# Folding keys into the query weights of four latent attentions, moving the mask test to other engines, and running batch 0's last attention inside the last decoder layer

## What is computed

```python
# L0 and L3 (softmax over the 512 tokens, not over the 77 keys)
q = x @ Wq + bq;  k = ctx @ Wk + bk;  v = ctx @ Wv + bv
w = softmax(q @ k.T / sqrt(128), axis=tokens)
x = layernorm(w @ v + x) * gamma + beta
# L1 (ordinary cross attention, one head)
x = x + softmax((x@Wq+bq) @ (ctx@Wk+bk).T / sqrt(128)) @ (ctx@Wv+bv) @ Wo + bo
# L2: six layers, 16 heads of 64
t = mha(ln(t), ln(t), self weights, mask 512 x 512) + t
t = mha(ctx, ln(t), cross weights, mask 77) + t
t = t + relu(ln(t) @ w1 + b1) @ w2 + b2
```

## Time and profile before

| | us |
|---|---|
| median of 3 runs | 1139.71 (1138.81 to 1141.12) |
| the profiled execution, whole | 1137.97 |
| its span, first to last instruction | 1136.1 |
| PE busy / ACT / DVE / POOL | 1043.2 / 773.5 / 751.3 / 385.2 |
| prologue, to the first decoder norm | 0 to 74.57 |
| one steady layer (out job at 224.81, next at 395.89) | 171.08 |
| last residual sum to the end | 1112.17 to 1136.1 |

### The profile page before, as it was taken

How to read it: one execution, slowest core, us unless ns; L and a number is a source line. 1 busy time by engine, 2 the same in 40 slices (tenths; PEclk the granted TensorE clock), 3 DMA queues, 4 the chain that set the end, 5 groups by cost and what they waited for, 6 DMA issues and landing times.

```text
span 1136.1 us, 21080 instructions
## 1 busy us (share of the span) xinstructions
PE 1043.2 (92%) x5374; PEld 659.5 (58%) x5374; DVE 751.3 (66%) x4546; ACT 773.5 (68%) x3453; POOL 385.2 (34%) x398
## 2 busy tenths in 40 slices
PE   5469999999999999999999999999999999999874
PEld 3346655656655656655656655666655666655532
DVE  2736578856678855678765678765678765678634
ACT  2128689856689856689856589856589856589821
POOL 2003344322344322354322354322354323354310
PEclk9659999999999999999999999999999999999987
DMA  8320110000410000310000410000410000000000
GB/s 240 50 70 1 51 33 1 1 1 11 115 33 2 1 1 2 121 35 1 2 1 1 121 37 2 1 1 2 121 36 1 2 1 1 20 1 1 1 0 19
DMA packets 37263, 32.45 MB, mean 29 GB/s; under 512 B 10768, under 2 KB 32528, under 8 KB 35984
## 3 DMA queue, kind: packets, MB, share of 16 engines
q1 hardware_dynamic: 37136, 31.03, 9.8%
HBM read 30.49 MB, written 0.52 MB: 27 GB/s over the span
## 4 chain that ended last, share of the span: by engine, by line
PE 83%; DVE 10%; issue 3%; ACT 2%; DVEq 1%; DMA 0%; SPq 0%
PE sum L856 23%; PE S L826 21%; PE T L836 11%; PE W L740 4%; PE W L682 4%; PE W L746 4%; PE W L669 2%; PE W L720 2%; PE W L699 2%; DVE Pb L1192 2%; PE W L735 2%; DVE XN L1045 1%; PE W L651 1%; PE W L660 1%; DVE stats L1034 1%
## 5 line engine op out<-in xcount | busy, mean ns | idle before, releaser
L986 ACT ACTIVATE Pb<-Pb,mn 128x128 f32<-128x128 f32 (+1 forms) x1536 | 560.9, 371 | 65.0 <-DVE mn L1192 65.0
L547 POOL TENSOR_TENSOR Pb<-Pb,rsum 128x512 f32<-128x512 f32 (+2 forms) x336 | 325.1, 969 | 600.6 <-DVE rsum L1200 600.1
L986 ACT ACTIVATION_READ_ACCUMULATOR Pb<-Pb,mn 128x1 f32 x1536 | 294.8, 192 | 0.0
L836 PEld LDWEIGHTS T<-ident,Pb 128*128 128x128 f32 (+2 forms) x1296 | 163.7, 147 | 153.9 <-issue 114.8
L1192 DVE CUSTOM_DVE_ANT_0 Pb<-S,late_bias 128x128 f32<-128x128 f32 x768 | 175.5, 285 | 110.5 <-PE S L826 109.8
L826 PE MATMUL S<-GV,XT 128*128 128x512 f32 x384 | 197.2, 600 | 1.4 <-DVE mn L1192 0.8
L836 PE MATMUL T<-ident,Pb 128*128 128x128 f32 (+2 forms) x1296 | 197.4, 273 | 0.0
L856 PE MATMUL sum<-PT,GV 128*128 128x512 f32 x384 | 192.4, 593 | 0.0
L1209 DVE COPY PT<-T 128x512 f32<-128x512 f32 (+1 forms) x240 | 157.3, 656 | 43.6 <-PE T L836 42.1
L1192 DVE CUSTOM_DVE_ANT_0 Pb<-S,cross_bias 128x77 f32<-128x77 f32 x768 | 132.4, 233 | 42.8 <-PE S L826 38.8
L856 PE MATMUL sum<-PT,Vc 128*128 128x512 f32 (+2 forms) x264 | 134.5, 599 | 0.0
(11 more groups left out here) (136 smaller groups left out, 1071.8 us busy)
## 6 DMA issues: line engine op xcount, KB each, us to landing
sakv<-in_L_xattn_sa_kv SPq DMA_DIRECT2D x6, 1024.0 KB, 5.3
caow<-in_L_xattn_ca_ow SPq DMA_DIRECT2D x132, 32.0 KB, 2.3
saq<-in_L_xattn_sa_q SPq DMA_DIRECT2D x6, 512.0 KB, 6.1
caq<-in_L_xattn_ca_q SPq DMA_DIRECT2D x6, 512.0 KB, 8.1
cakv<-in_L_xattn_ca_kv SPq DMA_DIRECT2D x6, 512.0 KB, 9.4
saow<-in_L_xattn_sa_ow SPq DMA_DIRECT2D x6, 512.0 KB, 4.2
w<-in_L_xattn_ff_w SPq DMA_DIRECT2D x12, 256.0 KB, 3.1
GV<-in_mask_BxSxS_ik SPq DMA_DIRECT2D x1, 2048.0 KB, 10.1
```

The costliest lines, as they stand in the source:

```text
L547: nc.gpsimd.tensor_tensor(rows, rows, r, ALU.mult).then_inc(sem(f"{unit.name}_weights"), 1)
L836: last = nc.tensor.transpose(T_ps[n % 2][0:k1 - k0, t * P:(t + 1) * P], Pb[:, n % SLOTS, k0:k1], ident[:])
L986: last = nc.scalar.activation(Pb[:, s, t * w:(t + 1) * w], Pb[:, s, t * w:(t + 1) * w], ACT.Exp, bias=mn[:, s, t:t + 1], scale=-1.0, accum ...
```

## The change

**Keys folded into the query weights.** For L0, L1 and L3, instead of q and then q times k, PE transposes `Wq` once and makes `G = Wq kT` (154 columns for both batches), scaled on ACT; the scores are one matmul of x with `G`. The part of the scores that comes from `bq` is one number per key (`key_biases`, `c_key`) or a row (`c_row`), added by DVE in the instruction that also takes the minimum (`token_least`, the same instruction as L1192). In L0 and L3 the softmax's divisor scales the 77 value rows in place of the 512-column weights. In L1 `Wo` is folded into the values (`vo["L1"]`) and the divisor is applied in the residual sum (`latent_residual`). L0's gamma and beta are applied to features by ACT's eviction; POOL makes the residual `X` from `XN` beside it.

**Batch by batch.** x is loaded in two DMAs, the norm runs per batch, L1's per-batch steps follow each other, and `latent_residual` stands behind the branch, as the decoder's first work on DVE.

**Mask test.** ACT squares the two blocks of the first 384 keys with a running sum, POOL makes `late_bias` from the integers, DVE keeps one minimum of 1024 numbers and a few small sums. The full bias is made in the general path only.

**Decoder.** L0's semaphore of eight loads becomes one per load, and the loads are issued in another order. `cq`, `ck`, `cv` and `cG` of layer 1 leave the prologue and become jobs of the first layer's self attention (`WEIGHTS0_AT`). `ck` and `cv` of a pair of heads are now made at once: the key weights stand in rows 0 to 63 of `cakv`, the value weights in rows 64 to 127, the context stands twice, and each job fills two banks. The 22 DMAs of `caow` become 9. The tables of ticks have other numbers.

**End.** L3's operands (`k3`, `v3`, `g3`) are jobs of the last layer; batch 0's scores to output (`x3`, `s3`, `exp3`, `scale3`, `p3`, norm `z`) run in the last cross attention and the last feed forward; only batch 1's stand after it.

```diff
-WEIGHTS = [("tq", i) for i in range(2)] + [("cq", i) for i in range(2)] + [("ck", i) for i in range(3)] \
-    + [("cv", i) for i in range(3)] + [("cG", i, r) for i in range(3) for r in range(2)]
+WEIGHTS = [("tq", i) for i in range(2)] + [("cq", i) for i in range(2)] + [(kind, i) for i in range(3) for kind in ("ck", "cv")] \
+    + [("cG", i, r) for i in range(3) for r in range(2)]
-WEIGHTS_AT = (26, 23, 31, 32, 30, 33, 33, 37, 38, 39, 40, 41, 42, 42, 45, 43)
+WEIGHTS_AT = (24, 23, 31, 32, 33, 33, 35, 35, 37, 37, 40, 40, 42, 42, 45, 44)
...
+    def last_attention(self, b, at, steps):
+        turned, scores, exps, scaled, values, norm = steps
+        self.jobs[at + turned].append(("x3", self.layers, b))
+        self.jobs[at + scores].append(("s3", self.layers, b))
+        self.late[at + exps].append(("exp3", b))
+        self.late[at + scaled].append(("scale3", b))
+        self.jobs[at + values].append(("p3", self.layers, b))
+        self.normalise(at + norm, ("z", self.layers, b, 3), (0, 0, 0))
...
+            if j + 1 == self.layers:
+                self.last_operands((s1 + 30, s1 + 31, s1 + 33))
+                self.last_attention(0, x1 + FEED0[1] + 4, LAST_AT)
+                self.last_attention(1, after + FEED1[1] + 4, LAST_AT)
...
+                elif what == "cv":
+                    i = event[2]
+                    keys = ("ck", j, i)
+                    fills, halves = [keys, event], [bank_of(ring, keys), w]
...
+                        for h in range(2):
+                            last = nc.tensor.matmul(halves[h][:, c * BM:(c + 1) * BM], cakv[half(h), p * P:(p + 1) * P],
+                                                    ctxT[half(h), :], start=True, stop=True)
...
+            pe.wait_ge(sem("L0_k_sb"), 1)
+            pe.wait_ge(sem("L0_wqT_sb"), 1)
+            nc.tensor.matmul(S_ps[0][:, 0:BM], wqTo["L0"][:], kTo["L0"][:].rearrange("p b m -> p (b m)"),
+                             start=True, stop=True).then_inc(sem("L0_G"), 1)
...
+            for i in range(2):
+                nc.scalar.activation(GV[:, 12 * i:12 * i + 4, 0:KEYS], full_bias[:, 4 * i:4 * i + 4, 0:KEYS].bitcast(I32),
+                                     ACT.Square, accum_out=unmasked[:, i:i + 1]).then_inc(sem("unmasked"), 1)
...
+                normalise(0, batch(b), XN, EPS_LATENT, "L0", b + 1)
+                if b == 1:
+                    normalise(2, batch(0), XN, EPS_LATENT, "L0", 1)
+                normalise(1, batch(b), XN, EPS_LATENT, "L0", b + 1)
...
+            def latent_residual(b):
+                dve.wait_ge(sem("L1_exp"), b + 1)
+                nc.vector.reciprocal(orec[:, batch(b)], osum[:, batch(b)])
+                dve.wait_ge(sem("X_biased"), b + 1)
+                dve.wait_ge(sem("L1_out"), b + 1)
+                dve.drain()
+                for t in range(TB):
+                    i = b * TB + t
+                    last = nc.vector.scalar_tensor_tensor(X[:, i, :], W_ps[b][:, t * P:(t + 1) * P], orec[:, i:i + 1],
+                                                          X[:, i, :], ALU.mult, ALU.add)
+                last.then_inc(sem("L1_done"), 1)
...
+                if unit is FAST:
+                    latent_residual(0)
                 for t in range(unit.ticks):
+                    if unit is FAST and t == 1:
+                        latent_residual(1)
```

637 lines of the change are left out of this document (384 added, 253 removed).

## The result

Over four executions the changed kernel took 1120.84 us in the median (1118.3 to 1123.13), the kernel before 1139.26 (1136.59 to 1141.12). The ratio is 0.9839, 95% interval 0.9809 to 0.987. The forecast was 1085.5 us with a range of 1073 to 1099, so the direction was right and the size wrong by a factor of three: 18.4 us were won, not 54.

What follows compares the result with a forecast made beforehand. TensorE was taken to bound the steady layers, a chain of hand-overs the prologue and end. −37.5 + 6 − 10 − 6.5 − 5.5 = −53.5 against 1137.97 gave 1084.5, stated as 1085.5 us; range 1073 to 1099.

Steps and rivals of the forecast that it cites:

- step 1: Prologue, up to L0's first residual sum: reached at 16.4 us instead of 21.75, a gain of 5.4.
- Step 2: Prologue, from the first residual sum to both batches' norm: 8.7 us for both, so done at 25.1.
- Step 3: Prologue, from the norms through the mask test to VectorE's flag: flag written at 29.3 us.
- Step 4: Prologue, branch to the decoder's first turn: at about 41 us instead of 78.45, −37.5 for the whole prologue.
- Rival (a): Prologue held by DMA, with L1's `bo` and ACT's squares behind the mask: 8 to 9 us later, 1094; chance 0.2.
- Layer 1 takes over work: First layer: cq, ck/cv and cG moved there add 5.5 to 7.0 us on full TensorE, taken as +6.
- Pairs: Five layers: key and value products made at once save 2.1 us a layer, −10 in all.
- Rival (b): Layers: waits for VectorE eat the gain, +15 in place of −6.5, 1107, or half of it, 1096; chance 0.12.
- Order: Five layers: new tick order removes TensorE's 1.61 us wait before the first cG; net 1.3 a layer, −6.5.
- End: After the last residual sum: only batch 1 remains, −8.3; batch 0's work inside the last layer +2.8; net −5.5.

Runs made afterwards that it cites:

- roots_first: Changed kernel with GpSimd taking both norm roots before the mask's last columns, and VectorE scaling batch 1 before reducing the mask: 1120.36 us.
- defer_loads: Changed kernel with the first layer's weight loads and the last attention's loads issued only after L1_done: 1119.52 us.
- best: padded_new_order with roots_first's edit, late loads held for L1_done and TensorE's branch, and TensorE's wait for L1_done behind its branch: 1106.36 us.
- padded_new_order: Changed kernel with key and value products one kind at a time, zero-padded to 128 rows, at the earlier kernel's ticks; other tables kept: 1114.5 us.
- experiment 3: Four variants of the changed kernel with key and value products one kind at a time, on 64 or zero-padded 128 rows, old or new order: 1114.5 to 1123.35 us.
- order_before: Changed kernel with the layers' tick tables back at the earlier kernel's numbers, pairs kept at ticks 30, 33 and 38: 1126.78 us.
- padded kernels: Changed kernel with key and value products one kind at a time, zero-padded to 128 rows; old order 1115.91 us, new order 1114.5 us.
- all_padded: Changed kernel with single zero-padded products, old layer tables, deferred loads, both roots first and TensorE's wait for L1_done behind its branch: 1113.91 us.
- fill_wait: Changed kernel with the first pair at tick 31 and 28 unused identity turns before TensorE's wait for XN of batch 0's hidden layer: 1120.34 us.

## Why the prediction was wrong, step by step

**Prologue, step 1** (16.4; measured 17.01): right.

**Step 2** (both norms by 25.1; measured 28.7): the step that failed is GpSimd's side. I had counted VectorE's minimum over the mask's 1024 columns, but not the 3.64 us in which GpSimd makes them, between its two roots. Beside GpSimd's work VectorE's scaling also took 1.27 + 1.93 us instead of 0.34 + 0.85. roots_first wins 1.3 us of it; the rest only changes places, since GpSimd's 3.64 us remain on the way to the flag.

**Step 3** (flag at 29.3; 33.68): late by step 2's 3.6 and 0.8 more, most of it VectorE's two adds of one column (L1313), 2.38 us here beside GpSimd's work and 1.73 in roots_first.

**Step 4** (first turn at 41; 52.52). Two errors. I moved the 4.28 us of the earlier trace rows as a constant; it is 4.1 us in defer_loads, beside quiet queues, and 8.4 here, beside full ones, and the change brought the branch forward from a stretch of DMA share 0.20 (the window 70 to 74 us of the kernel before) into one of 1.16. And I let TensorE's branch run beside VectorE's work, though the code makes it wait for `L1_done` first: 3.6 us. The sum: 4.4 + 4.1 + 3.6 = 12.1, less 0.6 of small gains, is the 11.5 that were missing. best gives back 6.5. Rival (a) had the size (8 to 9 us) and a wrong cause: ACT's squares began at 16.91, 0.9 later than I had taken, and of the loads only L1's `bo` held anything on the way to the flag, the first root by some 0.3 us.

**Layer 1 takes over work** (+6). TensorE's busy time grew by 6.9 us, inside the 5.5 to 7.0 of the step. What failed is the waits, which I had put at nothing. The stretch grew by 10.2 us: the other 3.3 are idle time of TensorE (8.2 us against 4.9), of which 2.2 are gone in padded_new_order (6.0 us idle, 154.7 in all), so they are the pairs'. The other 1.1 I can't place. In the kernel before the first 8 us of this stretch also ran at about half the clock and here they did not; a like stretch cost best 1.1 us against padded_new_order (155.8 and 154.7).

**Pairs** (-2.1 a layer): the step that failed most. TensorE's work fell by 1.0 us a layer (165.0 against 166.0), since a product's duration in the earlier trace rows is not its distance to the next, and each change between 64 and 128 rows costs. Against padded_new_order, with the same order and 165.7 us of work, the pairs save 0.7 us of work and add 1.3 of waits (the 1.95 us for VectorE's copies above all), for a layer 0.6 us longer (171.45 against 170.85); and behind these waits the clock fell in every second layer, 1.7 us each in this execution. Against padded_new_order the pairs cost 6.3 us in the median. Rival (b) had named the copies, with 3 us a layer; what the Trainium skill states on the drain (see experiment 3) spoke against the change, and I had not used it.

**Order** (-1.3 a layer). Beside the pairs it held in size: -0.9 in an undisturbed layer, and 5.9 us in the median against order_before, of the 6.5 forecast; part of the 5.9 is the clock, which stood in no step, so that this figure fits is partly luck. And it only makes good a part of what the pairs cost. Without them it is 0.0 in the steady layers and -1.0 in the last: the 1.61 before the first cG is gone beside the pairs, and 1.7 is there at the same place once the pairs are gone. A wait of TensorE for the chain oT, VectorE, GpSimd, XN isn't removed by ordering, only filled.

**End** (-5.5). Batch 1's part is right to 0.1 us (15.7 against 15.6). Batch 0's part was put at +2.8; the last layer got 1.5 us shorter, although TensorE's work in it grew by 1.1 (162.2 against 161.1), since its idle time fell from 7.5 to 4.8 us. The order alone is worth 1.0 of this by the padded kernels.

The clock stood in none of the steps. I read 1.00 in a steady layer and took it for a property of the layer; it fell behind the new waits, and in all_padded behind waits of the old sizes too.

## What to carry to other kernels

Price a group of small matmuls by the distance from its start to the next start, not by durations, and count two mode changes for each group that is tiled otherwise than its neighbours; a product padded with zeros can be the faster one. Before a branch or any jump into new code, look at the DMA queues, not only at the engine: hold back bulk loads until every engine that the path needs has jumped, and let no engine wait ahead of its jump for what it needs only behind it. Where TensorE must wait for a chain, look at neighbouring waits together, because what follows may run at the lower clock; if nothing useful fits, turns of the identity can fill a wait; in fill_wait they cost nothing. And when two parts of a change meet, undo each with the other in place and without it: the order was worth 5.9 us beside the pairs and almost nothing without them.
